# Layer one of a graph network on Trainium2: scaling on VectorE, 64 row fetches a round on ScalarE, and the last twelve groups as three rounds of four

## The chip, the cores and the metric

The kernel runs on one core of one Trainium2 chip. A core has five engines with queues of their own: TensorE (PE; its weight loads are PEld), VectorE (DVE), ScalarE (ACT), GpSimd (POOL) and SyncE (SP). They meet only through semaphores. The metric is the device time of one execution, in microseconds. Three executions of the kernel before took 3249.84, 3252.46 and 3268.34 us, median 3252.46.

## What is computed

Two layers of a graph network on 6250 nodes of 128 channels, with 106,250 edges sorted by receiver. Layer one is attention: the features of each edge's sender are weighted by a softmax over the receiver's edges, in four heads, and summed per receiver. Layer two passes each edge through small dense layers and sums again.

```python
x = nodes @ W + b_lin                                   # layer one
sent, recvd = x[snd], x[rcv]
logits = leaky_relu(sum(concat(sent, recvd) * alpha))   # per head
e = exp(logits - segment_max(logits, rcv)[rcv])
att = e / segment_sum(e, rcv)[rcv]
out = segment_sum(att * sent, rcv) + bias
...
ef = (relu(edge_attr @ We1 + be1) @ We2 + be2) * sigmoid(ts @ Wt + bt)   # layer two
msg = relu(concat(x[row], ef) @ Wn1 + bn1) @ Wn2 + bn2
out = segment_sum(msg, col) + x
```

## The kernel before

**Tiles, groups, rounds.** Edges are cut into 832 tiles of 128, four tiles are a group (208 groups), and layer one goes in rounds: `SPAN_SIZES` gives 4 groups, then 25 times 8, then 4, so 27 rounds, 0 to 26. `LAST` is the last round and `CLOSE` the one ahead of it. The sender's row of every edge (130 numbers: 128 features and 2 logits) is fetched from a table in memory by its index.

**Who fetches.** GpSimd gathers 128 rows with one instruction (line 439) into `rows0`, a ring of 24 groups; the slot of group g is free when `agg0` has counted group g - 24. SyncE fetches 17 whole tiles (`LINE_TILES`) row by row, one DMA each (line 386), into three slots of `rows_x`; ScalarE does the same for 6 tiles (`ACT_TILES0`, line 1104, 32 rows in a round, two slots in `rows_w`, which the profile names `moments`). Ahead of every 16 rows the issuing engine loads 16 offsets (line 108).

**A round of layer one.** ScalarE copies the logits of the round's tiles (`keep_logits`, lines 1052 to 1059). TensorE turns them (863). VectorE scans for the maximum of each receiver's run (593 to 619), with three small turns by TensorE between. ScalarE takes the exponential (1073), TensorE turns it back, ScalarE copies it to `edge_w` (1079). Then, group by group: TensorE sums the weights (903) and the weighted rows (909) with one-hot masks that VectorE makes two groups ahead (634), into PSUM, and counts `agg0`; VectorE adds the four tiles into the accumulators `acc2` at columns that the first receiver of each tile sets (639) and counts `acc0`. The rows are weighted on ScalarE, one activation for each tile and head, in place (`scale_group`, 1091). TensorE works at most two groups ahead of VectorE. Once in a round two factors (1084, 1085) rescale the running accumulators (629, 630).

**Order on ScalarE.** Exponential, copies, all the round's activations with the two factors after the first group, one `halo` load, then `fetch(r)`, then `keep_logits(r + 1)`. Whatever it waits for holds up all behind it.

**Order on VectorE.** `sum_group` for each group, with the penalties of the next round after the first group; every fourth group and once ahead of the scans `first_of` loads 16 column addresses from memory in SBUF to registers (623).

**The end of layer one.** From group 195 on receivers are complete. In `CLOSE` TensorE also turns the sums of weights block by block (925) and VectorE collects them (`gather_stats`, 683). In the last round maxima, `shares`, `scaled_sums` (712) and `mix` (718) finish the nodes, with GpSimd helping (445 to 455). SyncE writes them to a table for layer two. The scans of the last round lie inside the groups of `CLOSE` (`parts_after`).

**Layer two** goes group by group, with gathers by GpSimd (1297), row fetches by SyncE (16 tiles, line 1250, with the loads of `ea` and `ts` between them in the same queue) and by ScalarE (8 tiles). VectorE loads 16 addresses in every fourth group, before it waits for that group's sums.

## Time and profile before

| | |
|---|---|
| profiled execution | 3252.87 us, its span 3251.1 us |
| busy: PE, PEld | 1733.2 us (53%), 1190.2 us (37%) |
| busy: DVE, ACT, POOL | 1460.3 us (45%), 948.5 us (29%), 1557.9 us (48%) |
| mean granted TensorE clock | 0.688 |
| ACT activations of line 1091 | 1618, mean 312 ns, 359.2 us |
| PE line 909, rows times masks | 1618, mean 398 ns, 369.9 us |
| DMA packets | 113031, 213.29 MB |

A row of a timeline gives start, duration, engine, line and operation, what is written and read, and in brackets how long the engine had stood idle and what ended that. "issue" is idle time in which it waited for nothing that the profile shows, such as its own issue of DMAs. "remote" is a semaphore event that the profile gives to no instruction. SPq and ACTq rows are DMA issues. Layer one ends near 1646 us; the loop over its rounds begins near 196.

### The profile page before, as it was taken

Reading aid. Unit: us, or ns where it says so; the run is one execution under the profiler, and the core shown is the slowest. Engines: PE = TensorE matmul, PEld = TensorE weight load, DVE = VectorE, ACT = ScalarE, POOL = GpSimd, SP = SyncE. Lnnn points to the kernel's source line nnn. Section 1 sums busy time; section 2 is a strip of 40 time slices with the busy share of each in tenths; the row PEclk is TensorE's granted clock in tenths of the full one; section 3 lists DMA queues with packets and bytes.
Section 4 is the critical chain, followed back from the end, with each engine's and each line's share of the span. In section 5 each row is a group of like instructions: output and inputs, shape, how many; then the busy total and the mean of one; then the engine's idle time right before and its main releaser. Section 6 shows DMA issues by size and latency. Waiting matters only on the chain.

```text
span 3251.1 us, 44463 instructions
## 1 busy us (share of the span) xinstructions
PE 1733.2 (53%) x8785; PEld 1190.2 (37%) x8785; DVE 1460.3 (45%) x5237; ACT 948.5 (29%) x2832; POOL 1557.9 (48%) x1656
## 2 busy tenths in 40 slices
PE   2254544342433424344536666666667567666668
PEld 2243333232322323223434444334344344444446
DVE  2264554343433534344644444444444344444447
ACT  2352332231311313223244322222222222222223
POOL 5526556464544545451154544444554455445451
PEclk6666556565555655556658877777787777777779
DMA  4212112111111112110042323332323332333233
GB/s 119 60 23 47 43 43 45 31 45 32 44 32 32 44 33 45 32 45 13 12 124 65 100 72 92 93 95 75 94 78 93 91 90 84 92 93 96 74 96 110
DMA packets 113031, 213.29 MB, mean 66 GB/s; under 512 B 36223, under 2 KB 76580, under 8 KB 102773
## 3 DMA queue, kind: packets, MB, share of 16 engines
q0 software_dynamic: 51616, 106.59, 13.3%
q1 hardware_dynamic: 54921, 101.96, 10.9%
q10 hardware_dynamic: 6220, 1.91, 0.3%
q14 instruction: 202, 1.65, 0.2%
q8 instruction: 72, 1.18, 0.2%
HBM read 197.43 MB, written 12.88 MB: 65 GB/s over the span
## 4 chain that ended last, share of the span: by engine, by line
SPq 55%; issue 35%; PE 3%; DVE 3%; another core or an unknown queue 2%; ACT 1%; DMA 1%; POOL 0%; ACTq 0%; DVEq 0%; POOLq 0%
SPq L386 23%; SPq L1250 22%; SPq L108 8%; SPq L1246 1%; SPq L1245 1%; DVE acc L639 1%; PE pair L1354 0%; PE pair L1348 0%; PE bank L1363 0%; PE bank L1374 0%; PE bank L1332 0%; DVE moments L1477 0%; PE bank L1383 0%; DMA bias_ext<-in_b_lin 0%
## 5 line engine op out<-in xcount | busy, mean ns | idle before, releaser
L1297 POOL DMA_INDIRECT acc<-table,index x806 | 765.7, 950 | 781.7 <-DVE pre L1542 499.4
L439 POOL DMA_INDIRECT rows<-table,index x759 | 719.7, 948 | 701.5 <-PE pair L909 334.0
L634 DVE TENSOR_SCALAR onehot<-iota_row,dst_rel 128x128 f32<-128x128 f32 x832 | 243.6, 294 | 458.7 <-remote 387.2
L1348 PE MATMUL pair<-ea,we 64*128 64x512 f32 x416 | 273.3, 742 | 310.3 <-DMA ea<-in_ea_t 305.9
L1560 DVE TENSOR_TENSOR acc<-acc,bank 128x128 f32 x832 | 238.7, 287 | 331.6 <-remote 178.4
L909 PE MATMUL pair<-onehot,rows 128*128 128x128 f32 x1618 | 369.9, 398 | 0.0
L1091 ACT ACTIVATE rows<-rows,edge_w 128x32 f32<-128x32 f32 x1618 | 359.2, 312 | 36.4 <-issue 35.0
L1433 ACT ACTIVATE hidden<-pair,be 128x512 f32<-128x512 f32 x208 | 142.9, 687 | 717.3 <-PE pair L1348 277.7
L639 DVE TENSOR_TENSOR acc<-acc,pair 128x256 f32 x832 | 348.8, 419 | 1.5 <-issue 1.4
L909 PEld LDWEIGHTS pair<-onehot,rows 128*128 128x128 f32 x1618 | 319.4, 293 | 63.7 <-issue 54.8
L1354 PE MATMUL pair<-hidden,we 128*128 128x512 f32 x416 | 288.3, 781 | 95.2 <-ACT hidden L1433 87.0
L1363 PEld LDWEIGHTS bank<-wn1b,ef 128*128 128x128 f32 x1664 | 277.0, 238 | 163.7 <-issue 113.8
L1523 DVE SCALAR_TENSOR_TENSOR ef<-pair,be,gate 128x512 f32<-128x512 f32 x208 | 155.1, 746 | 330.1 <-PE pair L1354 239.8
L1363 PE MATMUL bank<-wn1b,ef 128*128 128x128 f32 x1664 | 280.4, 324 | 22.9 <-DVE ef L1523 22.9
L1374 PE MATMUL bank<-onehot,msg 128*128 128x128 f32 x1664 | 259.0, 306 | 47.0 <-ACT msg L1446 40.8
L903 PE MATMUL pair<-onehot,edge_w 128*5 128x128 f32 x1664 | 119.9, 378 | 296.8 <-DVE onehot L634 191.9
L1374 PEld LDWEIGHTS bank<-onehot,msg 128*128 128x128 f32 x1664 | 240.8, 223 | 52.6 <-ACT msg L1446 44.9
L1446 ACT ACTIVATE msg<-pre 128x512 f32<-128x512 f32 x208 | 130.6, 628 | 349.6 <-DVE pre L1542 284.0
L1348 PEld LDWEIGHTS pair<-ea,we 64*128 64x128 f32 x416 | 69.7, 209 | 342.2 <-DMA ea<-in_ea_t 314.7
L863 PE MATMUL bank<-ident,lg_cols 128*66 128x128 f32 (+1 forms) x27 | 11.2, 413 | 338.3 <-ACT lg_cols L1059 299.4
L1516 DVE TENSOR_SCALAR onehot<-iota_row,dst_rel 128x128 f32<-128x128 f32 x832 | 187.4, 290 | 0.1
L1542 DVE TENSOR_TENSOR pre<-bank,acc 128x512 f32<-128x512 f32 x184 | 125.6, 683 | 118.0 <-remote 65.4
(171 smaller groups left out, 1429.6 us busy)
## 6 DMA issues: line engine op xcount, KB each, us to landing
ts<-in_ts SPq DMA_DIRECT2D x52, 1024.0 KB
rows_x<-table SPq DMA_DIRECT2D x2176, 0.5 KB
rows_y<-table SPq DMA_DIRECT2D x2048, 0.5 KB
ea<-in_ea_t SPq DMA_DIRECT2D x52, 512.0 KB
rows_z<-table ACTq DMA_DIRECT2D x1024, 0.5 KB
acc<-table,index POOLq DMA_INDIRECT x806
moments<-table ACTq DMA_DIRECT2D x768, 0.5 KB
rows<-table,index POOLq DMA_INDIRECT x759
```

What stands on the lines that cost most here:

```text
L108: eng.load(regs, lines[j:j + 1, o:o + n])
L386: sp.dma_start(octets(rows_x[o + q:o + q + 1, j % LINE_SLOTS, :]), row_at(sp, bytes1, v, ROW1)).then_inc(line_in[j % LINE_SLOTS], 16)
L439: gp.indirect_dma_start(rows0[:, n % (RING * TG), :], None, table1, bass.IndirectOffsetOnAxis(index[:, n:n + 1], 0)).then_inc(half_in[g % ...
L639: dve.tensor_tensor(acc2[:, :, ds(v, P)], acc2[:, :, ds(v, P)], both_sums[n // TG % 2][:, :, n % TG * P:(n % TG + 1) * P], ALU.add).then_i ...
L909: last = pe.matmul(row_sums[g % 2][:, t * P:(t + 1) * P], row_of(g * TG + t)[:, 0:CH], onehot[:, g % 2, t, :], start=True, stop=True)
L1091: act.activation(row, row, ACT.Copy, scale=edge_w[:, r % 2, (g - SPANS[r][0]) * TG + t, h:h + 1]).then_inc(scaled0, 1)
L1250: sp.dma_start(octets(rows_y[o + q:o + q + 1, j % LINE_SLOTS, :]), row_at(sp, bytes2, v, ROW2)).then_inc(line1_in[j % LINE_SLOTS], 16)
L1297: gp.indirect_dma_start(rows[:, g % RG1, t, :], None, table, bass.IndirectOffsetOnAxis(index[:, n:n + 1], 0)).then_inc(gathered[g % RG1], 16)
L1348: pe.matmul(bank[g % 2][:, :], we1[:, :], ea[:, g // HALF % 2, edges(g)], start=True, stop=True).then_inc(h1, 1)
L1354: pe.matmul(bank[2 + g % 2][:, :], we2[:, :], hidden[:, g % 2], start=True, stop=True).then_inc(h2, 1)
L1363: last = pe.matmul(bank[4 + g % 2][:, t * P:(t + 1) * P], ef[:, g % 2, t * P:(t + 1) * P], wn1b[:, :], start=True, stop=True)
L1374: last = pe.matmul(bank[6 + g % 2][:, t * P:(t + 1) * P], msg[:, g % 2, t, :], onehot[:, g % 2, t, :], start=True, stop=True)
```

## The change

It does these things.

- *Scaling.* In rounds before `SHORT_TURNS` (rounds 0 to 24) VectorE weights the rows (`scale_rows`), one product for a whole group, or one for each piece where a tile lies in `rows_x` or `rows_w`. The first two groups of a round are done in `open_scaling`, once the weights are there, the others two groups ahead in `sum_group`. The last three rounds stay with ScalarE.
- *ScalarE's fetches.* `ACT_TURNS` is 2, so a tile takes two rounds of 64 rows, and there are 12 tiles instead of 6, from round 0 on. The 64 go in two halves with `halo` between. The third tile and later ones first wait for the first group of their own round.
- *Rounds.* Sizes are 4, 24 times 8, and 4, 4, 4: 28 rounds. `CLOSE` has four groups and no scan of the last round inside it; TensorE turns the sums of two blocks' groups after each of its groups.
- *Early masks.* The masks of the last six groups (202 to 207) have storage of their own and are made in the groups of round 24, three in each.
- *Early addresses.* `first_nodes` loads the addresses of a half ahead, in the second group of each four, in both layers.
- *The last chain.* The shares and the first scaled sums stand between the scans of the last round; `mix` moves one place ahead.

The core of the diff:

```diff
-SPAN_SIZES = [HALF] + [RG] * (ROUNDS - 1) + [HALF]
+SPAN_SIZES = [HALF] + [RG] * (ROUNDS - 2) + [HALF] * 3
-ACT_TURNS = 4
+ACT_TURNS = 2
-LAST, CLOSE = TURNS - 1, TURNS - 2
+LAST, CLOSE, SHORT_TURNS = TURNS - 1, TURNS - 2, TURNS - 3
+EARLY = range(GROUPS - 6, GROUPS)
...
+        def first_nodes(dve, name, g):
+
+            regs = [dve.alloc_register(f"{name}{g * TG + q}") for q in range(HALF * TG)]
+            dve.load(regs, dst_first[0:1, g * TG:(g + HALF) * TG])
+            return [dve.snap(v, donate=True, min_val=0, max_val=N) for v in regs]
...
+                def scale_rows(r, g):
+
+                    k = g * TG - SPANS[r][0] * TG
+                    for n, end in scale_parts(g):
+                        i = k + n - g * TG
+                        mine = rows_of(n, end)[:, :, 0:SH * HC].rearrange("p t (h c) -> p t h c", c=HC)
+                        dve.tensor_tensor(mine, mine, edge_w[:, r % 2, i:i + end - n, 0:SH].unsqueeze(3).broadcast_to([P, end - n, SH, HC]), ALU.mult).then_inc(scaled_v, 1)
+
+                def open_scaling(r):
+
+                    dve.wait_ge(ew_ready, 2 * (r + 1))
+                    for g in groups(r)[0:2]:
+                        scale_rows(r, g)
+
+                def sum_group(g, at, r=None):
+                    if r is not None and g + 2 in groups(r):
+                        scale_rows(r, g + 2)
                     dve.wait_ge(agg0, g + 1)
                     for t in range(TG):
-                        if g + 2 < GROUPS:
+                        if g + 2 < EARLY.start:
                             mask((g + 2) * TG + t)
...
+                def sum_half(k, g, r=None):
+
+                    if k % HALF == 1 and g + 2 * HALF - 1 < GROUPS:
+                        at[g + 2 * HALF - 1] = first_of(g + 2 * HALF - 1)
+                    sum_group(g, at[g - k % HALF][k % HALF * TG:(k % HALF + 1) * TG], r)
...
+                        if r == CLOSE - 1:
+                            for n in range((EARLY.start * RG + k * len(EARLY)) * TG // RG, (EARLY.start * RG + (k + 1) * len(EARLY)) * TG // RG):
+                                mask(n)
                     scan_rows(r)
                     scan_row_ends(r)
                     full_maxima(r)
+                    if r < SHORT_TURNS:
+                        open_scaling(r)
...
-                    if k >= 1:
-                        gather_stats(k - 1)
+                    gather_stats(2 * k)
+                    gather_stats(2 * k + 1)
                 g1 = SPANS[LAST][0]
-                at = first_of(g1)
-                gather_stats(7)
+                at = at[g1]
                 gather_stats(8)
                 maxima_of(0)
+                scan_rows(LAST)
+                shares(0)
+                scan_row_ends(LAST)
+                scaled_sums(0)
+                full_maxima(LAST)
+                scaled_sums(1)
                 dve.wait_ge(acc0, g1 * TG)
                 rescale(LAST, at)
-                shares(0)
                 sum_group(g1, at[0:TG])
-                scaled_sums(0)
+                mix(0)
...
-                def fetch(r):
-                    j, k = divmod(r - 1, ACT_TURNS)
-                    if r < 1 or j >= len(ACT_TILES0):
+                def fetch(r, half):
+                    j, k = divmod(r, ACT_TURNS)
+                    if j >= len(ACT_TILES0):
                         return
...
-                    if k == 0 and j >= 2:
+                    if k == 0 and half == 0 and j >= 2:
                         act.wait_ge(agg0, ACT_TILES0[j - 2] // TG + 1)
...
+                for r in range(SHORT_TURNS):
+                    exponentials(r)
+                    keep_weights(r)
+                    factors(r)
+                    fetch(r, 0)
+                    if r == 0:
+                        halo(2)
+                    if r + 3 < TURNS:
+                        halo(r + 3)
+                    fetch(r, 1)
+                    keep_logits(r + 1)
+                for r in range(SHORT_TURNS, TURNS):
+                    if r == LAST:
+                        shares_up(0)
```

How ScalarE's queue stands in one round of eight groups, in the middle of layer one. `moments` is the tile `rows_w`; x16 is sixteen row fetches. Before:

```order
L1079 COPY edge_w<-bank 128x2x32 x2
L1091 ACTIVATE rows<-rows,edge_w 128x32 x8
L1084 ACTIVATE factor<-bank 128x1
L1085 ACTIVATE factor_w<-bank 128x1
L1091 ACTIVATE rows_x<-rows_x,edge_w 128x32 x2
L1091 ACTIVATE rows<-rows,edge_w 128x32 x22
L1068 DMA dn<-in_dst_halo 66x130
L1091 ACTIVATE rows<-rows,edge_w 128x32 x32
L108 TENSOR_LOAD offsets
L1104 DMA moments<-table 1x520 x16
L108 TENSOR_LOAD offsets
L1104 DMA moments<-table 1x520 x16
```

And now, for a round at the same place (the lines are those of the changed kernel):

```order
L1124 COPY edge_w<-bank 128x2x32 x2
L1129 ACTIVATE factor<-bank 128x1
L1130 ACTIVATE factor_w<-bank 128x1
L109 TENSOR_LOAD offsets
L1150 DMA moments<-table 1x520 x16
L109 TENSOR_LOAD offsets
L1150 DMA moments<-table 1x520 x16
L1113 DMA dn<-in_dst_halo 66x130
L109 TENSOR_LOAD offsets
L1150 DMA moments<-table 1x520 x16
L109 TENSOR_LOAD offsets
L1150 DMA moments<-table 1x520 x16
```

All 64 activations of line 1091 are gone from the round, and four blocks of 16 fetches with their offset loads stand where two stood, the halo load in the middle.

VectorE's queue between the end of `CLOSE` and the first group of the last round, with the shares in it; `rows` here are the work arrays in the ring's free part. Before (698 to 705 are the shares, 629 and 630 the rescaling):

```order
L692 COPY count<-rows 128x34
L629 ISA
L629 TENSOR_SCALAR acc<-acc,factor 128x1
L630 ISA
L630 TENSOR_SCALAR acc<-acc,factor_w 128x1
L698 TENSOR_TENSOR rows<-rows 128x34x2
L699 TENSOR_TENSOR rows<-rows 128x34x2
L702 TENSOR_TENSOR rows<-rows 128x136
L703 RECIPROCAL rows<-rows 128x136
L704 TENSOR_TENSOR rows<-rows 128x136
L705 TENSOR_TENSOR rows<-rows 128x136
L634 TENSOR_SCALAR onehot<-iota_row,dst_rel 128x128
```

And now (742 to 749 are the shares):

```order
L742 TENSOR_TENSOR rows<-rows 128x34x2
L743 TENSOR_TENSOR rows<-rows 128x34x2
L746 TENSOR_TENSOR rows<-rows 128x136
L747 RECIPROCAL rows<-rows 128x136
L748 TENSOR_TENSOR rows<-rows 128x136
L749 TENSOR_TENSOR rows<-rows 128x136
L628 COPY edge_of<-bank 1x4x16
L630 SCALAR_TENSOR_TENSOR runs<-pens,edge_of 1x36
L631 SCALAR_TENSOR_TENSOR runs<-pens,edge_of 1x36
L633 TENSOR_TENSOR delta<-edge_of,runs 1x2
L635 TENSOR_SCALAR delta<-delta,same 1x2
L756 TENSOR_TENSOR rows<-bank,rows 128x256
```

The scans of the last round now stand here, the row ends (628 to 635) behind the shares and a scaled sum (756) behind them; before they stood between groups 3 to 6 of the `CLOSE` round, and behind the shares came at once the first mask of the last round's groups.

## Rows read from the trace of the kernel before

**Rows 1.** The page's chain of waits, by engine and by line.

```profile
SPq 55%; issue 35%; PE 3%; DVE 3%; another core or an unknown queue 2%; ACT 1%; DMA 1%; POOL 0%; ACTq 0%; DVEq 0%; POOLq 0%
SPq L386 23%; SPq L1250 22%; SPq L108 8%; SPq L1246 1%; SPq L1245 1%; DVE acc L639 1%; PE pair L1354 0%; PE pair L1348 0%; PE bank L1363 0%; PE bank L1374 0%; PE bank L1332 0%; DVE moments L1477 0%; PE bank L1383 0%; DMA bias_ext<-in_b_lin 
```

**Rows 2.** SyncE's row fetches of line 386: x count, ns min/median/max, first and last start.

```profile
L386 SPq DMA_DIRECT2D rows_x<-table x2176: 2/228/1398, 97.3 to 1568.1; - x198
```

**Rows 3.** Waits from 240 to 1580 us: total us, times, longest.

```profile
ACT lg_cols L1059 <- issue: 526.1, 24, 23.1
ACT lg_cols L1052 <- DMA rows_x<-table: 208.3, 8, 28.4
```

**Rows 4.** ScalarE's timeline, two rounds: start, us, operation, idle before and its releaser.

```profile
765.91 0.19 ACT L1052 COPY lg_cols<-rows_x 128x2 f32<-128x2 f32 x1 [28.39 <-DMA rows_x<-table]
770.80 0.31 ACT L1073 ACTIVATE weights<-shifted 66x128 f32<-66x128 f32 x1 [4.51 <-DVE shifted L618]
...
819.04 0.31 ACT L1073 ACTIVATE weights<-shifted 66x128 f32<-66x128 f32 x1 [9.03 <-DVE shifted L618]
822.86 0.17 ACT L1085 ACTIVATE factor_w<-bank 128x1 f32<-128x1 f32 x1
...
836.36 22.96 ACTq L1104 DMA_DIRECT2D moments<-table  x32
...
868.57 0.31 ACT L1073 ACTIVATE weights<-shifted 66x128 f32<-66x128 f32 x1 [8.48 <-DVE shifted L618]
```

**Rows 5.** SyncE's fetches counted in six stretches; last row a window (DMA share 0.22).

```profile
L386 SPq DMA_DIRECT2D rows_x<-table x26: 3/18/701, 836.9 to 859.2; - x26
L386 SPq DMA_DIRECT2D rows_x<-table x25: 3/16/708, 787.3 to 809.3; - x25
L386 SPq DMA_DIRECT2D rows_x<-table x16: 4/212/709, 824.8 to 836.1; - x16
L386 SPq DMA_DIRECT2D rows_x<-table x12: 6/15/700, 809.6 to 818.1; - x12
L386 SPq DMA_DIRECT2D rows_x<-table x45: 227/228/263, 747.5 to 764.7; - x45
L386 SPq DMA_DIRECT2D rows_x<-table x32: 227/228/270, 1536.8 to 1548.3; - x32
836.40:859.40 23.00, 10.14 (x64) 7.56 (x64) 8.51 (x32) 0.00 (x0) 14.52 (x17) 0.57 0.22 49
```

**Rows 6.** Timeline of ScalarE (first row) and VectorE in the tail.

```profile
1574.17 0.31 ACT L1073 ACTIVATE weights<-shifted 66x128 f32<-66x128 f32 x1 [4.50 <-DVE shifted L618]
...
1580.01 0.29 DVE L634 TENSOR_SCALAR onehot<-iota_row,dst_rel 128x128 f32<-128x128 f32 x1 [1.04 <-PE pair L909]
...
1618.71 0.41 DVE L639 TENSOR_TENSOR acc<-acc,pair 128x256 f32 x1
...
1643.28 0.56 DVE L718 TENSOR_TENSOR x_rows<-x_rows,rows 128x384 f32<-128x384 f32 x1
```

**Rows 7.** Layer two: SyncE's fetches of line 1250, and a wait of TensorE.

```profile
L1250 SPq DMA_DIRECT2D rows_y<-table x2048: 2/228/1397, 1718.1 to 3169.3; - x187
PE pair L1348 <- DMA ea<-in_ea_t: 305.9, 37, 17.4
```

**Rows 8.** Groups of instructions, 240 to 1500 us (busy, mean ns | idle, releasers); address loads.

```profile
L439 POOL DMA_INDIRECT rows<-table,index x689 | 653.3, 948 | 591.8 <-PE pair L909 280.3 <-issue 183.2 <-remote 128.3
L639 DVE TENSOR_TENSOR acc<-acc,pair 128x256 f32 x728 | 305.3, 419 | 0.9 <-issue 0.9
L623 DVEq TENSOR_LOAD <-dst_first x52: 1095/1099/1348, 196.2 to 1606.0; - x52
```

**Rows 9.** Timeline of VectorE and GpSimd where both resume together.

```profile
797.53 0.29 DVE L634 TENSOR_SCALAR onehot<-iota_row,dst_rel 128x128 f32<-128x128 f32 x1 [7.26 <-remote]
797.76 0.94 POOL L439 DMA_INDIRECT rows<-table,index  x1 [2.21 <-remote]
...
809.36 0.29 DVE L634 TENSOR_SCALAR onehot<-iota_row,dst_rel 128x128 f32<-128x128 f32 x1 [7.35 <-remote]
```

More of the change, by code:

```diff
@@ L263, in gnn_layers @@
                                  "delta_ready", "spread", "shift_ready", "top_ready", "w_ready", "w_turned", "ew_ready", "factor_done"))
-            oh0, scaled0, agg0, acc0 = (sem(n) for n in ("oh0", "scaled0", "agg0", "acc0"))
+            early_ready = sem("early_ready")
+            oh0, scaled0, scaled_v, agg0, acc0 = (sem(n) for n in ("oh0", "scaled0", "scaled_v", "agg0", "acc0"))
             half_in = [sem(f"half_in{s}") for s in range(RING // HALF)]
@@ L357, in ring_parts, with mask_of, scale_parts, scaled_until @@
                 return list(zip(cuts, cuts[1:]))
-            def parts_after(r):
-                return (3, 4, 5, 6) if r == LAST else ()
+            def mask_of(n):
+                i = n - EARLY.start * TG
+                if i < 0:
+                    return onehot[:, n // TG % 2, n % TG, :]
+                return early_a[:, i, :] if i < IN_PAIR else early_b[:, i - IN_PAIR, :]
+            def scale_parts(g):
+                n, end = g * TG, (g + 1) * TG
+                cuts = sorted({n, end, *(x + d for x in LINE_TILES + ACT_TILES0 for d in (0, 1) if n <= x + d < end)})
+                return list(zip(cuts, cuts[1:]))
+            def scaled_until(g):
+                return sum(len(scale_parts(v)) for v in range(g + 1))
+            def rows_of(n, end):
+                if n in LINE_TILES or n in ACT_TILES0:
+                    return row_of(n).unsqueeze(1)
+                return rows0[:, n % (RING * TG):n % (RING * TG) + end - n, :]
             def data_cols(v, r):
@@ L492, in first_vector @@
             def first_vector(dve):
-                regs = [dve.alloc_register(f"first0_{q}") for q in range(HALF * TG)]
                 dve.memset(stat_sums[0][:, :], 0.0).then_inc(set_done, 1)
@@ L621, in first_of @@
                 def first_of(g):
-                    dve.load(regs, dst_first[0:1, g * TG:(g + HALF) * TG])
-                    return [dve.snap(v, min_val=0, max_val=N) for v in regs]
+                    return first_nodes(dve, "first0_", g)
                 def rescale(r, at):
@@ L898, in sum_group @@
                         pe.wait_ge(ew_ready, 2 * (r + 1))
-                    pe.wait_ge(oh0, (g + 1) * TG)
+                    if g in EARLY:
+                        pe.wait_ge(early_ready, (g + 1 - EARLY.start) * TG)
+                    else:
+                        pe.wait_ge(oh0, (g + 1) * TG)
                     if g >= 2:
@@ L1106, in first_scalar @@
                 keep_logits(0)
-                for r in range(TURNS):
+                for r in range(SHORT_TURNS):
[12 more added lines that the diff above has]
+                        shares_up(0)
                     exponentials(r)
@@ L1114, in first_scalar @@
                             factors(r)
-                            if r == 0:
-                                halo(2)
-                            if r == LAST:
-                                shares_up(0)
-                        if k == HALF - 1 and r + 3 < TURNS:
-                            halo(r + 3)
-                        if r == CLOSE and k == parts_after(LAST)[0]:
-                            keep_logits(r + 1)
-                    fetch(r)
-                    if r < CLOSE:
+                    if r < LAST:
                         keep_logits(r + 1)
@@ L1507, in second_vector @@
                 dve.wait_ge(cleared, PARTS + 1)
-                regs = [dve.alloc_register(f"first1_{q}") for q in range(HALF * TG)]
+                at = {0: first_nodes(dve, "first1_", 0)}
                 dve.wait_ge(w1_in, 16 * 7)
@@ L1547, in add_sender @@
                         dve.tensor_tensor(pre[:, g % 2, 1:TG], z[:, 1:TG], rows[:, g % RG1, 1:TG], ALU.add).then_inc(radd, 1)
[L1549 removed]
                 def add(g):
[L1552 to L1554 removed]
+                    if g % HALF == 1 and g + HALF - 1 < GROUPS:
+                        at[g + HALF - 1] = first_nodes(dve, "first1_", g + HALF - 1)
                     dve.wait_ge(agg1, g + 1)
                     for t in range(TG):
[L1557 removed]
+                        v = at[g - g % HALF][g % HALF * TG + t]
                         if g or t:
```

88 lines of the change are left out of this document (35 added, 53 removed).

## Prediction, made before the changed kernel was run

> **What bounds the kernel now.** I read the page's chain of waits first. 55% of it is SyncE's queue (SPq), 23% the single-row fetches of line 386 in layer one, 22% those of line 1250 in layer two [rows 1]. The reader should see one queue with hardly a pause: 2176 row fetches of line 386, the last at 1568.1 us [rows 2]. The waits show who feels it. Eight times ScalarE stood still for a SyncE row tile before `keep_logits`, 208.3 us in all, 28.4 at most. The 526.1 us under "issue" before the same copies are ScalarE's own 24 blocks of 32 row fetches, about 23 us each [rows 3].
>
> So layer one has two kinds of round. One without a late tile is ScalarE's and VectorE's: exponential at 819.04, the next at 868.57, 49.5 us [rows 4]. One with a late tile is SyncE's: `lg_cols` at 765.91 came 28.39 us late and the exponential followed 4.9 us behind [rows 4]. Over the layer SyncE decides, since it never rests.
>
> How fast does SyncE issue? I counted its rows in stretches. While GpSimd gathers and ScalarE fetches: 26 rows in 23.0 us and 25 in 22.7, 0.90 us each. While GpSimd gathers and ScalarE does not fetch: 16 in 11.2 us and 12 in 9.8, 0.75 us each. With GpSimd quiet: 45 in 18.5 us and, with ScalarE fetching, 32 in 11.6; I take 0.40 us for both [rows 5]. The gathers halve SyncE's rate; ScalarE's fetches take a fifth more, but only under gathers.
>
> After 1568.1 follows a tail: the exponential of round 25 at 1574.17, VectorE's first mask in it 5.8 us later, when the first aggregate is there, and its last `x_rows` at 1643.28 + 0.56 [rows 6]. Layer two is again SyncE's: 2048 fetches from 1718.1 to 3169.3, with TensorE idle 305.9 us for `ea` loads that stand in the same queue [rows 7].
>
> **The change part by part.** Times are against the profiled execution (3252.87 us, span 3251.1), 0.4 us from the median of 3252.46.
>
> *Scaling moves to VectorE.* Per round of eight groups ScalarE loses 64 activations; the fetch now starts right behind `factor_w`. VectorE gains eight products of 256 elements, 0.42 us each by the accumulation of that size (0.419), plus 0.28 for each piece cut off for a single tile: 4 us a round [rows 8]. Cover: VectorE stands idle some 7.3 us twice a round [rows 9]. Without that cover it would cost 25 x 4 = 100 us. Nothing by itself.
>
> *64 rows a round by ScalarE.* 768 more row fetches. First its own floor. From the exponential to `factor_w` 4.0 us; two halves of 23.0 (under gathers, as now) with a halo issue between, about 0.5; then 4.9 from the first copy to the exponential where VectorE is free: 55.4 [rows 4]. In every second round the fetch also waits for the first group of its own round (`agg0` of the tile whose slot it overwrites), 5.8 us after the exponential [rows 6] instead of 4.0. That makes 56 to 58; I take 57. It is 7.5 us over 49.5, in 23 rounds 173 us, but those hide in the 208 us that ScalarE now waits for rows. From the first exponential near 196, with 48 for the short round 0, 23 x 57, and 30 for round 24 without a fetch, round 25 could start at 1585.
>
> Second, SyncE. Gather time in the 1328 us from 240 to 1568: 653.3 busy, plus 183.2 and 128.3 between gathers of one run, 965 us [rows 8]. ScalarE fetches in 505 of them (526.1 less the two blocks after the last gather). Rows now: 505 / 0.90 + 460 / 0.75 + 363 / 0.40 = 561 + 613 + 907 = 2081. After: six gathers less, 957 us, all under fetches: 1063 rows; the other 1018 cost 407 us. 957 + 407 = 1364, 36 us more. SyncE's last row comes at 1604 and round 25 starts at 1610, after ScalarE's 1585. SyncE stays the bound: **+36**. If the fetch cost it nothing (0.75) the floor of 57 would set 1585, +11; if ScalarE needed 60 us a round, its bound would be 1654, +80. Between these ends I go by the windows, the nearest rows.
>
> The Trainium skill has a rule against reading this as a cost of issue (DMA: Bandwidth & Descriptors, "Issuing engines are not separate DMA queues"): all issuers end on the same 16 DMA engines and interleave, and a second issuer only saves issue time. In the fetch windows those engines are 0.22 busy, so by that rule SyncE would lose nothing, and the sum would be 3252.9 + 11 + 12 = 3276; by the rows it is 3301.
>
> *Tile slots, SyncE's order.* ScalarE's tiles go from 6 to 12, all six taken from GpSimd, none from SyncE, whose 17 tiles and order stay. Per gather 1.25 us, 7.5 in all, counted above.
>
> *Early addresses.* The load of 16 addresses, 1.1 us and its moves (1.3), leaves the stretch between the last accumulation and `scan_rows` [rows 8]. In ScalarE's rounds that is hidden behind the longer fetch, in SyncE's behind the wait for the row. In layer two it moves within VectorE's queue while SyncE bounds: 0, at most 52 x 1.3 = 68 us if VectorE were the bound, which the 305.9 us behind loads exclude.
>
> *Tail.* Now 69.7 us from the exponential of round 25 to the last `x_rows` [rows 6]. After, with durations from VectorE's and TensorE's timeline of the same stretch, round 25 has four groups: 5.8 to its first aggregate, four groups at 2.2 with their masks, penalties 1.7, addresses 1.3, scan chain 4.4: 22. Round 26, also four: 5.5, then TensorE paces it, since it turns two blocks of sums a group (0.6 + 2.1 + 2 x 1.1 = 4.9 at the lower clock, about half at the higher; I take 3.7), three more groups 11; the last additions, `gather_stats(8)` and the maxima 4.5; the scans, shares and carries in one stretch 6: 27. Last round: 5.5 and 5 to its third group, from there the 25.1 that it takes now (1618.71 to 1643.84), less 0.7 for a product moved ahead and 2 because GpSimd gets its shares earlier: 33. Sum 82, **+12**. The early masks save 24 x 0.21 = 5 (in it); they are made in round 24's groups while the row tile of group 197 is awaited. One more serial chain costs 10, a second one 6. Bounds: -5 if TensorE runs fast and the shares come free, +20 at the lower clock.
>
> Sum: 3252.9 + 36 + 12 = **3301 us**.
>
> **Rivals.**
> - *ScalarE does not slow SyncE (chance 0.22).* SyncE's rate would be set by the gathers alone. For it: with GpSimd quiet SyncE takes 0.36 us a row under ScalarE's fetch and 0.41 without it, so the two issue queues do not slow each other there. Against: 0.90 against 0.75 under gathers [rows 5]. Then ScalarE's floor decides: 3252.9 + 11 + 12 = 3276, within 1%. The rule of the Trainium skill above ends here.
> - *ScalarE becomes the bound (0.10).* At 0.77 us a row of its own instead of 0.72 (22.96 / 32) a round takes 60 us and round 25 starts at 1654: 3252.9 + 80 + 12 = 3345. It takes over from 58.1 us a round, where its bound passes 1610. For it: every one of its rows now lies under gathers. Against: the block of 32 took 22.96 us with gathers running all through [rows 4].
> - *Faster (0.17).* What slows SyncE under gathers might be ScalarE's dense work of any kind, its activations with a semaphore each among them. Gathers come in runs of eight, after which GpSimd and VectorE resume on an `agg0` that came 2.1 and 7.3 us late, 12 us apart, two groups at a time [rows 9]. If the activations hold that count back and slow SyncE, both end with them. A run of 31 gathers takes 39 us instead of 44, 22 x 5 = 110 us less in all; ScalarE's round shrinks to 54 (its last ten rows at 0.40), round 25 could start at 1516; SyncE at 0.75 would be done before (847 / 0.75 = 1129 rows, 952 more in 381 us, end at 1468). 3252.9 - 58 + 12 = 3207. It decides once round 25 starts before 1530. For it: `agg0` comes late also while ScalarE only scales. Against: the stretch with scaling is SyncE's better one under gathers (16 rows in 11.2 us, against 12 in 9.8 without) [rows 5].
> - *The rest (0.51)* is the forecast, 3276 to 3320.
>
> **Numbers.** Within 1% (32.5 us, about what a measurement of this kernel can tell from no change) lie the first rival (0.22), the lower edge of the forecast (0.07) and a little of the faster one (0.01): 0.30. Slower by over 1%: 0.44 + 0.10 = 0.54. Faster: 0.16. Range 3232 to 3345: it leaves out the faster case and the upper half of the ScalarE-bound one. The forecast's own range is 3276 to 3320.
>
> **What would show it.** SyncE's last single-row fetch of layer one near 1604 and never pausing; about 0.90 us a row through all gather stretches; exponentials 56 to 58 apart where no row tile is late, and ScalarE's wait for row tiles shrunk from 208 to some 75 us. VectorE's products 0.42 us each with no wait in TensorE on them. From the exponential of round 25 to the last `x_rows` some 82 us. Layer two, from its first gather to the end, as now within 10 us. The prediction is wrong if SyncE's count per us stays at 0.75 under fetches, if the runs of gathers get shorter than 44 us a round, or if layer two moves.

## The result, and the profile after

The changed kernel takes 3275.36 us (median of 20 runs, 3261.82 to 3289.61), the kernel before beside it 3252.77 us. The ratio of the runs is 1.0049, with a 95% interval of 1.0035 to 1.0064: 16 us slower, where 48 were forecast (the two medians alone are 23 us apart). The profiled executions are 3269.74 and 3252.87 us, 16.9 us apart, and that difference splits as follows.

| stretch, us | before | after | change | forecast |
|---|---|---|---|---|
| to the exponential of round 25 | 1574.2 | 1605.3 | +31 | +36 |
| from there to the end of the last `x_rows` | 69.7 | 81.2 | +12 | +12 |
| from there to the end of the span (layer two) | 1607.3 | 1581.4 | -26 | 0 |

The page of the kernel after, its chain of waits and two groups (busy, mean ns | idle before, releaser):

```profile
SPq 50%; issue 32%; PE 5%; another core or an unknown queue 5%; DVE 4%; ACT 2%; ACTq 2%; DMA 1%; POOL 0%; DVEq 0%; POOLq 0%
SPq L1300 22%; SPq L415 20%; SPq L109 7%; ACTq L1150 1%; DVE acc L666 1%; PE pair L960 1%; SPq L1296 1%; SPq L1295 1%; PE pair L1398 1%; PE pair L1404 1%; ACT normed L1048 1%; PE bank L1424 1%; PE bank L1413 0%; DMA ea<-in_ea_t 0%
...
L1347 POOL DMA_INDIRECT acc<-table,index x806 | 765.1, 949 | 757.8 <-DVE pre L1592 455.5
L1398 PE MATMUL pair<-ea,we 64*128 64x512 f32 x416 | 274.1, 744 | 276.7 <-DMA ea<-in_ea_t 276.7
```

It is still one queue: SyncE's row fetches are line 415 (386 before) and line 1300 (1250 before). Both lists run from first to last start without a pause: in layer one no two starts are more than 4.2 us apart, in layer two none more than 9.6. Layer one's now ends at 1599.8 instead of 1568.1 [rows 2]. Layer two's takes 1428.9 us instead of 1451.2, and TensorE waits 276.7 us for `ea` instead of 305.9 [rows 7].

```profile
L415 SPq DMA_DIRECT2D rows_x<-table x2176: 3/228/1437, 97.3 to 1599.8; - x198
L1300 SPq DMA_DIRECT2D rows_y<-table x2048: 2/228/1395, 1759.4 to 3188.3; - x187
```

Two rounds of ScalarE's timeline, SyncE's rows counted in the two fetch stretches of the second, and two waits of layer one (us in total, times, longest):

```profile
604.84 0.31 ACT L1118 ACTIVATE weights<-shifted 66x128 f32<-66x128 f32 x1 [4.51 <-DVE shifted L646]
608.66 0.17 ACT L1130 ACTIVATE factor_w<-bank 128x1 f32<-128x1 f32 x1
611.91 22.48 ACTq L1150 DMA_DIRECT2D moments<-table  x32
636.26 21.39 ACTq L1150 DMA_DIRECT2D moments<-table  x32
662.67 0.31 ACT L1118 ACTIVATE weights<-shifted 66x128 f32<-66x128 f32 x1 [4.52 <-DVE shifted L646]
...
L415 SPq DMA_DIRECT2D rows_x<-table x23: 4/17/701, 612.1 to 632.9; - x23
L415 SPq DMA_DIRECT2D rows_x<-table x23: 3/228/709, 637.0 to 657.3; - x23
...
ACT lg_cols L1104 <- issue: 1003.3, 23, 49.3
ACT lg_cols L1097 <- DMA rows_x<-table: 136.7, 7, 38.6
```

The reader should see a round of 57.8 us made of two blocks of 32 fetches, and SyncE at 23 rows in some 22 us beside each, 0.95 us a row. These are slow stretches of a long round. Where no row tile is late, the rounds whose fetch first waits for the first group take 55 to 58 us and those between them 47 to 53. Over the layer, by my count of the trace, a row of SyncE took 0.85 us beside ScalarE's fetches under gathers, and 0.89 us over all the time with gathers (0.85 in the kernel before). ScalarE's wait for SyncE's row tiles is down from 208.3 to 136.7 us, since its own fetches fill the time [rows 3]. The tail's two ends:

```profile
1605.25 0.31 ACT L1118 ACTIVATE weights<-shifted 34x128 f32<-34x128 f32 x1 [3.94 <-DVE shifted L646]
...
1685.93 0.56 DVE L762 TENSOR_TENSOR x_rows<-x_rows,rows 128x384 f32<-128x384 f32 x1
```

### The profile page after: what moved, and what is told of

It is laid out like the page before. It is cut to its first block, busy times and chain, and to the rows that moved or that the text cites. A ratio compares the mean times of both kernels' runs of the same rounds, so it can differ in the third digit from the quotient of the medians.

```text
span 3267.9 us, 44564 instructions
## 1 busy us (share of the span) xinstructions
PE 1763.1 (54%) x8804; PEld 1208.8 (37%) x8804; DVE 1546.0 (47%) x5496; ACT 604.2 (18%) x1282; POOL 1553.3 (48%) x1650
## 4 chain that ended last, share of the span: by engine, by line
SPq 50%; issue 32%; PE 5%; another core or an unknown queue 5%; DVE 4%; ACT 2%; ACTq 2%; DMA 1%; POOL 0%; DVEq 0%; POOLq 0%
SPq L1300 22%; SPq L415 20%; SPq L109 7%; ACTq L1150 1%; DVE acc L666 1%; PE pair L960 1%; SPq L1296 1%; SPq L1295 1%; PE pair L1398 1%; PE pair L1404 1%; ACT normed L1048 1%; PE bank L1424 1%; PE bank L1413 0%; DMA ea<-in_ea_t 0%
## 5 line engine op out<-in xcount | busy, mean ns | idle before, releaser
L1347 POOL DMA_INDIRECT acc<-table,index x806 | 765.1, 949 | 757.8 <-DVE pre L1592 455.5
L1398 PE MATMUL pair<-ea,we 64*128 64x512 f32 x416 | 274.1, 744 | 276.7 <-DMA ea<-in_ea_t 276.7
L661 DVE TENSOR_SCALAR onehot<-iota_row,dst_rel 128x128 f32<-128x128 f32 x808 | 238.1, 295 | 376.3 <-remote 323.8
L960 PE MATMUL pair<-onehot,rows 128*128 128x128 f32 x1558 | 379.1, 416 | 0.0
L960 PEld LDWEIGHTS pair<-onehot,rows 128*128 128x128 f32 x1558 | 326.1, 308 | 63.2 <-issue 61.6
L1104 ACT COPY lg_cols<-rows 128x2 f32<-128x2 f32 (+8 forms) x65 | 14.3, 232 | 1044.0 <-issue 1039.4
L1566 DVE TENSOR_SCALAR onehot<-iota_row,dst_rel 128x128 f32<-128x128 f32 x832 | 184.8, 287 | 0.1
```

What stands on the lines that cost most here:

```text
L661: dve.tensor_scalar(mask_of(n), iota_row[:, :], dst_rel[:, n:n + 1], None, ALU.is_equal).then_inc(early_ready if n // TG in EARLY else oh0, 1)
L960: last = pe.matmul(row_sums[g % 2][:, t * P:(t + 1) * P], row_of(g * TG + t)[:, 0:CH], mask_of(g * TG + t), start=True, stop=True)
L1347: gp.indirect_dma_start(rows[:, g % RG1, t, :], None, table, bass.IndirectOffsetOnAxis(index[:, n:n + 1], 0)).then_inc(gathered[g % RG1], 16)
L1398: pe.matmul(bank[g % 2][:, :], we1[:, :], ea[:, g // HALF % 2, edges(g)], start=True, stop=True).then_inc(h1, 1)
```

## The experiments

The kernels of one set ran on one chip; chips differ (the kernel before took 3253 to 3313 us), so ratios are to the kernel before of the same set, and stretches are compared within a set, or between the first and the third, which had the same chip. A stretch is read from one trace: kernels with the same code in layer one differ there by up to 13 us (`m_few` 1566.0, `m_fourth` 1579.0), those with the same code in layer two by some 5 (1614.3, 1616.7 and 1619.4 on the chip of the first set). "Layer two" below is the end of the span less the end of the last `x_rows`.

### First set: the addresses of layer two

`a_l2old` is the changed kernel with layer two's addresses as before. The other three are the kernel before with one part of that edit:

```diff
 # b_l2early
 def add(g):
-    if g % HALF == 0:
-        dve.load(regs, dst_first[0:1, g * TG:(g + HALF) * TG])
-        at[0] = [dve.snap(r, min_val=0, max_val=N) for r in regs]
+    if g % HALF == 1 and g + HALF - 1 < GROUPS:
+        at[g + HALF - 1] = first_nodes(dve, "first1_", g + HALF - 1)   # no copies
 # b_l2donate: if g % HALF == 0: at[g] = first_nodes(dve, "first1_", g)
 # b_l2moved: as b_l2early, with the load and the copies of before
```

> The changed kernel with the addresses of layer two loaded as before (at the head of each four groups, copied register by register), everything in layer one as changed. Theory E (the early addresses in layer two give the 26 us that the forecast lacks): span end less last x_rows of layer one back from 1581 to 1607 us, time 3301, ratio to before 1.013 to 1.016. Rival R (layer two is shorter for another reason: the place of tiles in memory, or the state in which layer one leaves the queues): layer two stays at 1581, ratio 1.004 to 1.007.

> The kernel before with only the addresses of layer two loaded early (in the second group of each four, for the next four, without copies). Theory E: layer two from the last x_rows to the end 1581 instead of 1607, time 3227, ratio 0.990 to 0.993, faster than both kernels. Rival R: no change, ratio 0.998 to 1.002.

> The kernel before; addresses of layer two loaded at the old place, but used from the loaded registers without the 16 copies. If the copies (0.23 and 0.16 us a load at least, as register operations on VectorE) are what E is about: all or most of the 26 us, ratio 0.990 to 0.995. If it is the place of the load (1.1 us between two accumulations while TensorE's aggregate is waited for): ratio 0.998 to 1.002.

> The kernel before; addresses of layer two loaded early, in the second group of each four, but still copied. The counterpart of the run before: if the place of the load counts, ratio 0.990 to 0.995; if the copies count, 0.998 to 1.002. Under rival R 0.998 to 1.002 in both.

| | place of the load | copies | ratio, interval | layer two, us |
|---|---|---|---|---|
| `a_l2old` | first of four | yes | 1.0152 (1.0127 to 1.0177) | 1646.0 |
| `b_l2donate` | first of four | no | 0.9989 (0.9973 to 1.0006) | 1642.3 |
| `b_l2early` | second of four | no | 0.9953 (0.9938 to 0.9968) | 1626.3 |
| `b_l2moved` | second of four | yes | 0.9904 (0.9882 to 0.9926) | 1614.3 |

SyncE's fetches of layer two, in the table's order: 1490, 1487, 1470 and 1456 us from first to last.

```profile
L1300 SPq DMA_DIRECT2D rows_y<-table x2048: 3/228/1411, 1780.4 to 3270.7; - x187
```

```profile
L1256 SPq DMA_DIRECT2D rows_y<-table x2048: 3/228/1413, 1738.3 to 3225.1; - x187
```

```profile
L1256 SPq DMA_DIRECT2D rows_y<-table x2048: 2/228/1479, 1746.9 to 3216.8; - x187
```

```profile
L1250 SPq DMA_DIRECT2D rows_y<-table x2048: 2/228/1487, 1736.2 to 3191.9; - x187
```

So the early addresses are where the missing 26 us are. With them undone the change costs 1.5%, as theory E had it and as the two terms of layer one foresaw (48 of 3253 us), and its layer two is as long as that of the kernel before on this chip (1646.0 us; 1645.1 in `b_double` of the third set, which turned out to be the kernel before). Done alone they make the kernel before faster. It is the place that counts; dropping the copies alone is no measurable change, and the early load is better with them than without (28 against 16 us of layer two). The expectation for `b_l2early` was nearly twice too large.

### Second set: ScalarE's rows, two tiles of SyncE, another place

```diff
 # a_32, from the changed kernel
-ACT_TURNS = 2
+ACT_TURNS = 4
 # m_t15, from b_l2moved: two of SyncE's seventeen tiles of layer one left to GpSimd
-LINE_TILES = [... (..., 85, 101, 109, 117, 133, 141, 157, 165, 181, ...)]
+LINE_TILES = [... (..., 85, 101, 117, 133, 141, 157, 181, ...)]
 # m_third, from b_l2moved
-    if g % HALF == 1 and g + HALF - 1 < GROUPS:
+    if g % HALF == 2 and g + HALF - 2 < GROUPS:
```

`after_again` is the changed kernel once more.

> The changed kernel itself, beside the kernel before on the same chip: the base for the run with 32 rows a round. Expected ratio 1.003 to 1.007, as in its own comparison (1.0049); exponential of round 25 some 31 us later than in the kernel before, last x_rows 12 us later still, layer two some 26 us shorter.

> The changed kernel with 32 rows a round by ScalarE as before (six tiles instead of twelve, fetched in four rounds each); VectorE still scales, three short rounds at the end stay. Theory S (ScalarE's fetches slow SyncE while GpSimd gathers): SyncE's last row and the exponential of round 25 come 30 us earlier than in the changed kernel, ratio 0.994 to 0.997. Rival C (ScalarE's fetches don't slow SyncE; the 31 us come from VectorE's scaling or something else that stays): no change, ratio 1.003 to 1.007. Rival D (less dense activations shorten the runs of gathers): exponential more than 40 us earlier.

> The kernel before with the addresses of layer two early (copied) as in b_l2moved, and two of SyncE's seventeen row tiles of layer one (groups 109 and 165) given to GpSimd. If SyncE's queue bounds layer one, as the forecast has it: 256 rows fewer at 0.61 us, SyncE's last row near 1440, and the exponential of round 25 goes from 1594 to 1450 at the earliest (24 rounds of 50 us, the next bound), ratio 0.95 to 0.965. Rival: GpSimd or the chain of VectorE and ScalarE bounds it as much as SyncE, and the late tiles only take up slack: exponential less than 40 us earlier, ratio above 0.98.

> As b_l2moved (ratio 0.9904), but the addresses of the next four groups are loaded in the third group of four instead of the second. If what costs is the old place, at the first group of four, ahead of the wait for its aggregate: 0.988 to 0.993 here too. If the second group is a lucky phase: 0.996 to 1.002.

| | ratio, interval | exponential of round 25 | tail | layer two |
|---|---|---|---|---|
| `after_again` | 1.0068 (1.0040 to 1.0097) | 1611.5 | 80.7 | 1595.1 |
| `a_32` | 0.9890 (0.9853 to 0.9926) | 1560.5 | 81.2 | 1585.7 |
| `m_t15` | 0.9614 (0.9586 to 0.9643) | 1476.8 | 68.0 | 1582.0 |
| `m_third` | 1.0000 (0.9978 to 1.0021) | 1575.3 | 70.2 | 1614.3 |

The exponentials of round 25, in the same order:

```profile
1611.46 0.31 ACT L1118 ACTIVATE weights<-shifted 34x128 f32<-34x128 f32 x1 [3.94 <-DVE shifted L646]
```

```profile
1560.52 0.31 ACT L1118 ACTIVATE weights<-shifted 34x128 f32<-34x128 f32 x1 [3.94 <-DVE shifted L646]
```

```profile
1476.79 0.31 ACT L1073 ACTIVATE weights<-shifted 66x128 f32<-66x128 f32 x1 [4.50 <-DVE shifted L618]
```

```profile
1575.32 0.31 ACT L1073 ACTIVATE weights<-shifted 66x128 f32<-66x128 f32 x1 [4.51 <-DVE shifted L618]
```

`m_third` has layer one as before. Against it the 64 rows come apart from the rest: with 32 rows, what `a_32` keeps of the change up to round 25 (VectorE's scaling, ScalarE's fetch right behind the exponentials, the early addresses of layer one) makes it 15 us *shorter*, and the 768 further rows of ScalarE make it 51 us longer. That was more than theory S asked for (30), and rival C, the first rival of the prediction, is out. The 51 us also pass the 40 of rival D, but its mechanism isn't there: the runs of gathers are no shorter in `a_32` than in `after_again` (43.1 and 42.6 us a round, by my count). The 15 us are hardly more than the scatter between traces; the third set bears them out. The Trainium skill (DMA: Bandwidth & Descriptors, "Issuing engines are not separate DMA queues") says that DMAs from all issuers run on the same 16 DMA engines and interleave, and that several issuers save only issue time; it gives no price for the sharing. The prediction read it, with those engines 0.22 busy, as no loss for SyncE; here SyncE loses 51 us to 768 rows, and the measurement decides.

`m_t15` says directly that SyncE bounds layer one: 98 us for 256 rows. It is less than expected (1477 instead of 1450), and three rounds still wait for a tile. The time with gathers stays (973 us in `m_third`, 975 here, by my count), so the rows that go come out of the time when GpSimd is quiet, where a row is cheap: 851 rows in 356 us there, 609 in 255 here, 0.42 us each. `m_third` was a miss for the theory that only the old place is bad: the third group is no better than the first.

### Third set: doubled loads, the old tail, thirteen tiles

```diff
 # b_double at the old place, m_double in b_l2moved's
+    dve.load(regs, dst_first[0:1, g * TG:(g + HALF) * TG])
     dve.load(regs, dst_first[0:1, g * TG:(g + HALF) * TG])
 # a32_oldtail, from a_32: the last twelve groups as before
-SPAN_SIZES = [HALF] + [RG] * (ROUNDS - 2) + [HALF] * 3
+SPAN_SIZES = [HALF] + [RG] * (ROUNDS - 1) + [HALF]
-EARLY = range(GROUPS - 6, GROUPS)
+EARLY = range(GROUPS, GROUPS)
 # and rounds CLOSE and LAST on VectorE, TensorE and ScalarE from the kernel before
 # m_t13, from b_l2moved
+LINE_TILES = [... (21, 29, 37, 53, 69, 85, 93, 109, 125, 141, 157, 173, 189)]
```

> The kernel before with the load of 16 addresses in layer two made twice at its old place (51 times 1.1 us more on VectorE, 57 us in all). Theory H (at the old place VectorE's 1.3 us lie partly on the path of a set of four groups): 15 to 40 us slower, ratio 1.004 to 1.012. Rival P (SyncE alone bounds layer two, and what an early load moves is only by chance how gathers and row fetches fall): ratio 0.997 to 1.003.

> As b_l2moved (ratio 0.9904), with the load in the second group of four made twice. There VectorE stands behind the wait for the set's edge attributes and ahead of an aggregate that TensorE hasn't finished. Theory H: the second load lies in that wait, ratio 0.988 to 0.993 as with one. Rival Q (the place is no better, 1.1 us there cost as much as anywhere): 0.998 or more. Rival P: any value.

> As a_32 (0.989), but with the last twelve groups as before: one round of eight and one of four, no early masks, shares and sums in their old places, two banks in their old order; VectorE scales up to the round of eight. The forecast's tail term is 12 us: from the exponential of round 25 to the last x_rows 70 us instead of 81, ratio 0.984 to 0.987. Rival T (the three short rounds cost nothing by themselves and the 12 us come from VectorE's scaling or the early masks in the rounds ahead): 80 us, ratio 0.988 to 0.990.

> As m_t15 (0.9614), with thirteen of SyncE's seventeen row tiles, about one in two rounds, at groups 21, 29, 37, 53, 69, 85, 93, 109, 125, 141, 157, 173 and 189. Each is fetched at least 15 us before ScalarE asks for it if a tile takes 94 us. Then no round waits for SyncE, and layer one runs at the 49.8 us a round of the other chain: exponential of round 25 from 1477 to 1420, ratio 0.942 to 0.95. Rival: GpSimd, with 43.5 us of gathers in a round of 49.8, or SyncE with tiles slowed by more gathers, keeps rounds late: above 0.955.

| | ratio, interval | exponential of round 25 | tail | layer two |
|---|---|---|---|---|
| `b_double` | 1.0013 (0.9992 to 1.0034) | 1594.8 | 68.8 | 1645.1 |
| `m_double` | 0.9914 (0.9886 to 0.9943) | 1596.8 | 68.6 | 1619.4 |
| `a32_oldtail` | 0.9888 (0.9856 to 0.9919) | 1568.3 | 67.7 | 1622.1 |
| `m_t13` | 0.9421 (0.9390 to 0.9452) | 1435.6 | 70.2 | 1616.7 |

The two doubled kernels tested nothing of the kind. Their traces have 52 loads each in layer two, as before: the load whose result is overwritten did not reach the program that ran. They are repeats of the kernel before and of `b_l2moved`, and agree with them. What the length of the load costs stays open.

```profile
L1554 DVEq TENSOR_LOAD <-dst_first x52: 1096/1099/1151, 1776.3 to 3289.1; - x52
```

`a32_oldtail` brings the tail back to 67.7 us, from 81.2 in `a_32`; its two ends:

```profile
1568.27 0.31 ACT L1128 ACTIVATE weights<-shifted 66x128 f32<-66x128 f32 x1 [4.51 <-DVE shifted L648]
...
1635.39 0.56 DVE L764 TENSOR_TENSOR x_rows<-x_rows,rows 128x384 f32<-128x384 f32 x1
```

The tail term is shown in its size. The ratio (0.9888, expected 0.984 to 0.987) isn't told apart from `a_32`'s, so there it is a miss, though the kept trace is of a run 10 us below the median: layer two, 23 us shorter than in `b_double` of the same set, gains less from the early load than in `a_32` (29 us against `m_third`). Its exponential, 27 us ahead of the two with the old layer one, agrees with `a_32` that VectorE's scaling and what goes with it help; which part of it does was not tried.

`m_t13` takes 159 us off layer one with 512 rows. One round of 74 us is left; no other takes over 52.

### Fourth and fifth set: what bounds each layer

```diff
 # m_few, from b_l2moved: 39 of 51 loads left out, those groups add at the first addresses
-    if g % HALF == 1 and g + HALF - 1 < GROUPS:
+    if g % HALF == 1 and 160 <= g + HALF - 1 < GROUPS:
 # m_fourth, from b_l2moved
-    if g % HALF == 1 and g + HALF - 1 < GROUPS:
+    if g % HALF == 3 and g + HALF - 3 < GROUPS:
 # t13_s16, from m_t13: SyncE's tiles of layer two every 16 groups; t13_s20: every 20, none in the last four groups
-LINE_STEP = 12
+LINE_STEP = 16
 # t13_a16, from m_t13
-ACT_TURNS = 4
+ACT_TURNS = 8
 # a_t13_s16: the changed kernel with LINE_TILES of m_t13 and LINE_STEP = 16
```

> As b_l2moved (0.9904), with 40 of the 51 later loads of addresses in layer two left out: the groups up to 159 then add at the first set's addresses, so that part of the sum is not what the reference computes; only the time is of use. If a load in the second group of four is as good as none: 0.988 to 0.993. If VectorE's load still costs something there: below 0.985. If it is the load in the second group that helps (it shifts what follows in a good direction): 0.996 to 1.002.

> As b_l2moved, with the load in the fourth group of four, one step ahead of the old place and still ahead of the wait for edge attributes. If any place but the second group costs the same as the old one: 0.997 to 1.002, as in the third. If the old place alone is bad and the third group was the exception: 0.988 to 0.993.

> As m_t13 (0.9421), with SyncE's row tiles of layer two every sixteen groups instead of twelve: twelve tiles instead of sixteen, so 512 rows go to four gathers. If SyncE's queue bounds layer two, as the forecast has it and as TensorE's 300 us behind edge attributes say: 512 rows at 0.70 us, 360 us less at most, until the next bound (GpSimd's 1040 us of gathers, VectorE's groups of some 5.5 us, 1150); at least 150 us shorter, ratio below 0.90. Rival: gathers, scaled by the port or the queues they share with the rows, are the real bound: less than 60 us, ratio above 0.925.

> As m_t13, with ScalarE fetching 16 rows a round instead of 32 (three tiles instead of six; 11.5 us less a round on ScalarE, three gathers more). If ScalarE's time bounds the rounds of 50 us that no row tile delays: exponential of round 25 more than 60 us earlier, ratio below 0.925. If GpSimd's runs of gathers (44 us a round with 32 of them) and VectorE's chain behind them bound: less than 25 us, ratio 0.934 to 0.944.

> The changed kernel with thirteen of SyncE's tiles in layer one and twelve in layer two, as t13_s16 (0.8912) has them. SyncE no longer bounds layer one. The forecast's floor for ScalarE with 64 rows a round is 57 us a round and 1585 us for the exponential of round 25: then 171 us later than in t13_s16 (1414), with 12 us of tail ratio 0.947 (0.942 to 0.955). Rival: ScalarE's rows get faster when SyncE fetches less (0.55 us a row), round 50 to 52 us, exponential before 1500, ratio below 0.925.

> As t13_s16, with SyncE's tiles of layer two every twenty groups: nine instead of twelve, 384 rows fewer and three gathers more. If SyncE still sets the pace of 26.2 us for four groups there: layer two shorter by up to 384 x 0.7 = 270 us, until TensorE (busy 0.77 of the stretch already) fills it at about 1270; some 80 us or more, ratio below 0.87. Rival: with twelve tiles the bound has already passed to TensorE, VectorE and ScalarE: less than 30 us, 0.882 or more.

| | ratio, interval | exponential of round 25 | tail | layer two |
|---|---|---|---|---|
| `m_few` | 0.9958 (0.9941 to 0.9974) | 1566.0 | 68.1 | 1600.2 |
| `m_fourth` | 1.0002 (0.9984 to 1.0019) | 1579.0 | 68.0 | 1618.1 |
| `t13_s16` | 0.8912 (0.8889 to 0.8934) | 1413.9 | 68.6 | 1417.8 |
| `t13_a16` | 0.9425 (0.9398 to 0.9451) | 1424.3 | 71.2 | 1581.1 |
| `a_t13_s16` (fifth set) | 0.9152 (0.9130 to 0.9173) | 1486.4 | 81.0 | 1418.0 |
| `t13_s20` (fifth set) | 0.8898 (0.8870 to 0.8927) | 1413.9 | 69.8 | 1414.2 |

*Place of the load.* The fourth group is as bad as the first and third. With most loads gone (`m_few`: 13 loads in its trace instead of 52; its ratio lies between two expectations) layer two takes 1600 us, but a load in the second group gives 1581 (`t13_a16`, whose layer two is `b_l2moved`'s, same set). That `t13_a16` differs in layer one should not matter: `m_t13` and `m_double`, which differ in the same way, have layers two of 1616.7 and 1619.4 us. The ratios say the same (0.9958 here, 0.9904 for `b_l2moved`), and the additions at the first addresses take no other time (286 ns against 287 in `m_fourth`). A load that were merely hidden in the second group would equal no load. It does better, so both "on VectorE's path" and "hidden" fall as the whole story.

*SyncE bounds layer two.* `t13_s16` takes 512 rows from SyncE and layer two shrinks from 1581 to 1418 us, as expected. TensorE's wait for `ea` falls from 305.9 [rows 7] to 61.8 us (waits of `t13_s16`). With nine tiles instead of twelve (`t13_s20`) nothing more is gained, as its rival had it, and the chain of waits no longer has line 1250 among its first lines. With twelve it still has it first, with 16%; so about there the bound passes to the other engines.

```profile
L1250 SPq DMA_DIRECT2D rows_y<-table x1536: 3/228/1462, 1555.7 to 2813.8; - x192
PE pair L1348 <- DMA ea<-in_ea_t: 61.8, 22, 9.0
```

The chain of waits of `t13_s20`:

```profile
issue 22%; DVE 18%; another core or an unknown queue 17%; PE 17%; SPq 14%; ACT 5%; ACTq 5%; DVEq 2%; POOL 0%; DMA 0%; POOLq 0%
```

*ScalarE's own floor.* In `a_t13_s16` SyncE no longer holds ScalarE back; four exponentials and three of the blocks between them:

```profile
982.94 0.31 ACT L1118 ACTIVATE weights<-shifted 66x128 f32<-66x128 f32 x1 [4.52 <-DVE shifted L646]
...
988.02 15.83 ACTq L1150 DMA_DIRECT2D moments<-table  x32
...
1030.64 0.31 ACT L1118 ACTIVATE weights<-shifted 66x128 f32<-66x128 f32 x1 [4.51 <-issue]
...
1037.72 22.95 ACTq L1150 DMA_DIRECT2D moments<-table  x32
1062.52 20.54 ACTq L1150 DMA_DIRECT2D moments<-table  x31
...
1088.25 0.31 ACT L1118 ACTIVATE weights<-shifted 66x128 f32<-66x128 f32 x1 [4.51 <-DVE shifted L646]
...
1139.00 0.31 ACT L1118 ACTIVATE weights<-shifted 66x128 f32<-66x128 f32 x1 [4.52 <-DVE shifted L646]
```

Some 57 us come only in every second round, where the fetch first waits for the first group; the others take 48 to 51, since their first block starts 5.1 us behind the exponential and takes 16 to 17 us. The mean from round 1 on is 51.9. So the rival's numbers came (its 0.55 us a row holds only in the rounds between): my floor of 57 for every round was 99 us too high over the layer (1486, not 1585). Against `t13_s20` of the same set the change still costs: ratio 0.9152 to 0.8898, 72 us in layer one and 11 in the tail.

*Rounds that no row tile delays.* With half of ScalarE's rows gone (`t13_a16`) most stay at 49.5 to 51, and the exponential of round 25 comes 10 us later than in `t13_s16`. ScalarE waits 388.0 us for VectorE's `shifted`. Their 50 us are not ScalarE's; whether GpSimd's runs of gathers or VectorE's chain set them wasn't tried.

```profile
ACT weights L1073 <- DVE shifted L618: 388.0, 19, 25.9
```

The fastest of the runs is `t13_s20` with 2899.37 us; `t13_s16`, with 2900.47 in its set, is not told apart from it.

## Why the prediction was right and wrong

**The total.** The changed kernel took 3275.4 us, and the first rival had said 3276. That is luck: the rival had +11 in layer one and 0 in layer two, the runs showed +31 and -26, and its mechanism (ScalarE's fetches don't slow SyncE) is the one that `a_32` rules out.

**SyncE bounds layer one: right.** It never pauses, its last row came at 1599.8 (forecast 1604), and 256 and 512 rows fewer took 98 and 159 us off. A row taken away saves 0.38 us, not the mean of 0.61, since it comes for the most part out of the quiet time; at 512 rows only 0.31, since there SyncE is done early (last row at 1396.4, exponential of round 25 at 1435.6) and another chain bounds.

**+36 for SyncE's pace: right in the sum (+31), in its parts helped by luck.** I counted SyncE's rows from 240 us to the exponential of round 25, with gathers less than 3 us apart as one stretch:

| us a row | under gathers | GpSimd quiet |
|---|---|---|
| forecast, before and after | 0.82, 0.90 | 0.40, 0.40 |
| `before`, `after` | 0.85, 0.89 | 0.42, 0.43 |
| `m_third`, `a_32`, `after_again` | 0.86, 0.82, 0.90 | 0.42, 0.41, 0.43 |

So the price under gathers came out near the forecast, and the 768 rows cost more all the same: 51 us by `after_again` against `a_32`, of which the time with gathers gives back 12 (forecast 8) and the quiet time takes 63 (forecast 44). The scaling, costed at "Nothing by itself", was off the other way together with the early addresses of layer one: 15 us shorter in the second set, 27 in the third. The two errors cancel, and that was luck. How the scaling or the addresses do it is open; a row under gathers is cheaper with them (0.86 to 0.82 us in the second set, 0.88 to 0.82 in the third). That bears on the rival "faster", but its condition, shorter runs of gathers, didn't come: 42.4 us a round before, 42.6 after. VectorE's products took 0.42 us each, as costed.

**ScalarE's floor of 57 us: too high by some 7 us in every second round,** as `a_t13_s16` shows. It did no harm to the sum, since SyncE bounds; ScalarE's wait for row tiles fell to 136.7 us and not to 75. The rival in which ScalarE becomes the bound is out with it.

**Tail +12: right.** 81.2 us against 82 forecast, +11.6 measured, and 13.5 less with the old tail (other chip). Its three rounds, from one exponential to the next and the last to the end, took 20.5, 25.5 and 35.2 us (forecast 22, 27 and 33).

**Layer two 0: the step that failed.** The prediction said: "In layer two it moves within VectorE's queue while SyncE bounds: 0". Its premise holds: SyncE bounds layer two. Its conclusion does not: layer two came 26 us shorter, and the edit is the cause (with it undone the ratio is 1.0152 instead of 1.0049, which is 33 us, and alone it takes 16 to 28 us off layer two in the first set). The hidden assumption was that a queue that bounds has a pace of its own. [rows 5] had shown that it hasn't: 0.40 us a row with GpSimd quiet, 0.75 to 0.90 under gathers, and most of GpSimd's idle time in layer two ends on VectorE's `pre`, as the 455.5 us on line 1347 say. In the first set, counted in the same way over layer two, a row of SyncE under gathers took 0.98, 0.97, 0.94 and 0.92 us in the table's order, for 990 to 1020 us with gathers in each. So an edit on VectorE can change the pace of a queue that it never touches. The count is no full account: in the fourth set `t13_a16` has 0.86, but `m_few` and `m_fourth` both 0.90 with layers two 18 us apart. Why the second group of four is the good place, better than no load, is not settled. I put the bound of 68 us aside with the words that the waits on `ea` exclude it; the range should have kept half of it, on the side of a gain.

## What to carry over

When one queue bounds a kernel, ask what sets that queue's pace, and cost at more than nothing whatever shifts the work that slows it. Here a row taken from the queue saved about what rows cost in its quiet stretches (0.38 us), not the mean. Before moving work between the engines around such a queue, try to take work from it: here eight row tiles of 33 handed back to GpSimd, together with the early load, made the kernel before 11% faster, while the change moved SyncE's bound the wrong way. Look in the trace whether an edit is there at all before reading its time.

## What the runs showed of the hardware

Under GpSimd's gathers SyncE's single-row fetches do not slow evenly. In layer two of the kernel before, by my count, 313 of 1044 starts with gathers running come 0.3 us or less after the last, 237 after 0.7 to 0.8, 261 after 1.4 to 1.6, and 74 after 2 us or more (a load of addresses stands ahead of every 16 rows). With GpSimd quiet 761 of 1003 come after 0.3 us or less. ScalarE's fetches under the same gathers add to SyncE's cost (51 us for 768 rows), though the two issue from queues of their own, ACTq and SPq in the rows.
